# Linear attention: the inverse normaliser in three stacked bf16 parts, its spread as one bf16 product, later spread and projection steps, and the mix matrix in two banks

## The chip, the cores and the metric

The kernel runs on one core of one Trainium2 chip. The metric is the device time of one execution, in microseconds. The kernel before was run three times: 3094.87, 3097.4 and 3097.8 us, median 3097.4 us.

## What is computed

The program is a stack of eight sublayers over 2048 tokens of width 128. The change touches the first one alone, linear attention with 16 heads of 64 columns:

```python
x = x + _layernorm(_L0_attn_ref(_layernorm(x, axis=-1), ...), axis=-1)

q = split_heads(x @ Wq); k = split_heads(x @ Wk); v = split_heads(x @ Wv)
q = jax.nn.elu(q) + 1.0
k = jax.nn.elu(k) + 1.0
k_sum = k.sum(axis=2)
z = jnp.einsum('bhnd,bhd->bhn', q, k_sum)[..., None] + EPS
kv = jnp.einsum('bhnd,bhne->bhde', k, v)
out = jnp.einsum('bhnd,bhde->bhne', q, kv) / z
return out.transpose(...).reshape(...) @ Wo + bo
```

## The kernel before

Each sublayer is a phase: its own buffers and semaphores, a barrier before and behind, and between two phases a short layer norm phase. Every engine runs its instructions in the order in which they are written, and waits on semaphores. All rows of the first phase lie between 19 and 209 us of the span.

The phase (`linear_attention_phase`, from line 415) handles two batches of 1024 tokens one after the other. A batch has two stages.

**Keys and values.** For each tile of 128 tokens, TensorE multiplies by Wk (L471) and Wv (L475) into four banks `proj`, ScalarE makes exp and relu, VectorE the features, and TensorE adds key by value into `outer` (L486). GpSimd sums the keys (L650).

**Queries.** A step counter u runs over 16 units (2 halves of 512 tokens by 8 chunks of 128 feature columns, two heads in each). In the order of its step, TensorE issues up to four things, each for another unit:

- `query` (L523), u < 16: one 128x512 product into `proj` bank 0 or 1. It waits until ScalarE has read the bank two units earlier.
- `normaliser` (L535), 3 steps later: the feature sums by the key sums, which gives z for the 16 heads, in rows 32j to 32j+15 for token group j. Half 0 goes to the bank `outer`, half 1 to `small`.
- `spread` (L551), 12 steps later: z's inverse, kept in `wide`, is copied to the 64 rows of each head by a product with a 0/1 matrix `select`, into `proj` bank 2 or 3. Unit u waits until VectorE has consumed unit u-2.
- `project_out` (L566), 13 steps later: four 128x128 products of the divided features `qz` with the matrix `mix` (kv by Wo) into `yacc`.

`mixes` (L510) makes the two halves of `mix` in steps 2 and 3, both in the one bank `small`, so that the second waits for VectorE's copy (L724) of the first. In step 19 of batch 0 TensorE also makes the first keys and values of batch 1.

VectorE's steps: query features (L673), in steps 10 and 18 the inversion of a half (`invert`: add epsilon L678, reciprocal L681, four copies of 16 rows into the diagonal blocks of `wide` L685), `divide` from step 12 on (L692: `qz` = features by the spread bank), `keep_y`, and in batch 1 pieces of the layer norm of batch 0. ScalarE makes exp and relu of each query (L617, L618). GpSimd has nothing in the query stage but two roots for the layer norm.

`select` and `wide` are f32 with 128 rows. The two places that order the work:

```python
for u in range(STEPS + 13):
    ...
    if 12 <= u < STEPS + 12:
        spread(b, u - 12)
    if u >= 13:
        project_out(b, u - 13)
```

## Time and profile before

| | |
|---|---|
| three runs | 3094.87, 3097.4, 3097.8 us |
| span of the profiled execution | 3093.3 us |
| its own time | not given apart from the span; the nearest run is 1.6 us above the span, the median 4.1 us |
| TensorE busy (products) | 2694.2 us, 87% |
| VectorE busy | 2049.2 us, 66% |
| ScalarE busy | 1572.2 us, 51% |
| GpSimd busy | 1072.5 us, 35% |
| mean granted TensorE clock | 0.938 |

How to read the rows further down. A row of a timeline has its start in us from the span's start, the duration in us, engine (PE is TensorE, DVE is VectorE, ACT is ScalarE, POOL is GpSimd), line, operation, output and inputs, shapes, and the count of merged records; in brackets the idle time of the engine just before, and what ended it. An f32 product shows as two records. Recorded ends of products overlap the next start; the distance of two starts is what a product costs in a stream. A row of the stretches has start and end, length, then for PE, weight loads, DVE, ACT and POOL busy us and count, and then the granted clock as a share of full speed, the DMA share and GB/s.

### The profile page before, as it was taken

How to read it: one execution, taken by the hardware profiler on the slowest of the kernel's cores; microseconds unless marked ns; L12 is line 12 of the kernel's file. 1: busy time of each engine (PE TensorE's matmuls, PEld its weight loads, DVE VectorE, ACT ScalarE, POOL GpSimd, SP SyncE). 2: the span in 40 equal slices, each digit the busy share in tenths (PEclk: the TensorE clock that was granted, in tenths of full speed). 3: DMA queues.
4: the chain of work that ended last, by engine and by line, in shares of the span. 5: the costliest groups of instructions: out<-in, count | busy, mean ns of one | idle time of the engine just before them, and what ended most of it. 6: DMA issues, size and time to landing. Idle time of an engine off the chain costs nothing. (4 is left out here: it accounts for less than half of the span.)

```text
span 3093.3 us, 55201 instructions
## 1 busy us (share of the span) xinstructions
PE 2694.2 (87%) x21256; PEld 1684.6 (54%) x21276; DVE 2049.2 (66%) x4308; ACT 1572.2 (51%) x3080; POOL 1072.5 (35%) x784
## 2 busy tenths in 40 slices
PE   8985899999799799999998888898877899777698
PEld 4552555566676566666666566465543334335465
DVE  5668999935644665546664665566439999996554
ACT  4334788852423444434554555366456676643122
POOL 3201000001243344434443553245226777773000
PEclk9995899989899899999999899998999999998899
DMA  1000000001120200000000000000013344340000
GB/s 55 1 4 1 2 3 3 3 2 82 33 89 22 84 1 1 1 1 1 1 1 1 29 1 1 1 1 1 1 66 129 137 144 144 136 143 21 1 1 14
DMA packets 34228, 105.41 MB, mean 34 GB/s; under 512 B 3456, under 2 KB 14592, under 8 KB 33200
## 3 DMA queue, kind: packets, MB, share of 16 engines
q1 hardware_dynamic: 31952, 97.69, 9.1%
q0 software_dynamic: 2016, 4.19, 0.4%
q8 instruction: 171, 2.80, 0.4%
q14 instruction: 89, 0.73, 0.1%
HBM read 94.01 MB, written 7.86 MB: 33 GB/s over the span
## 5 line engine op out<-in xcount | busy, mean ns | idle before, releaser
L2121 POOL TENSOR_TENSOR many_probs<-many_probs,many_rinv 128x2048 f32<-128x2048 f32 (+7 forms) x128 | 269.6, 2106 | 358.8 <-DVE many_rinv L2161 358.8
L1101 DVE TENSOR_REDUCE heads_halfmax<-heads_qmajor 128x1 f32<-128x512 f32 x512 | 316.3, 681 | 32.7 <-PE heads_qmajor L962 29.4
L3509 DVE TENSOR_TENSOR_SCAN stream_state<-stream_decay,stream_state 128x512 f32<-128x512 f32 x256 | 306.3, 1233 | 0.9 <-ACT stream_decay L3341 0.5
L1066 ACT ACTIVATE weights<-heads_kmajor 128x1024 f32<-128x1024 f32 x256 | 259.2, 1026 | 71.7 <-PE heads_kmajor L974 65.7
L2090 ACT ACTIVATE many_probs<-many_score,many_negmax 128x1024 f32<-128x1024 f32 (+7 forms) x256 | 187.4, 737 | 173.1 <-DVE many_negmax L2145 173.1
L2145 DVE TENSOR_REDUCE many_negmax<-many_score 128x1 f32<-128x1024 f32 (+7 forms) x256 | 184.4, 751 | 106.0 <-PE many_score L2019 104.3
L3179 PE MATMUL stream_yacc<-stream_state,ident 128*128 128x512 f32 x512 | 249.1, 614 | 0.4 <-POOL stream_state L3471 0.4
L3341 ACT ACTIVATE stream_decay<-weights,mamba_negA 128x512 f32<-128x512 f32 x256 | 173.0, 689 | 112.5 <-DVE stream_state L3509 111.3
L3471 POOL TENSOR_TENSOR stream_state<-XN,stream_state 128x1024 f32<-128x1024 f32 x85 | 200.2, 2359 | 81.6 <-DVE stream_state L3509 81.2
L2027 PE MATMUL many_ring<-ident,many_probs 128*128 128x128 f32 x1152 | 174.6, 279 | 23.4 <-POOL many_probs L2121 6.5
L3500 DVE TENSOR_TENSOR stream_state<-stream_bspread,stream_du 128x1024 f32<-128x1024 f32 x128 | 153.2, 1197 | 46.6 <-POOL stream_du L3447 38.6
L2080 ACT ACTIVATE many_probsT<-many_ring 128x512 f32<-128x512 f32 x192 | 107.8, 561 | 137.2 <-PE many_ring L2027 137.0
L990 PE MATMUL heads_outp<-weights,heads_vaug 128*9 128x128 f32 x4096 | 161.2, 276 | 13.5 <-ACT heads_outT L1059 13.2
L2027 PEld LDWEIGHTS many_ring<-ident,many_probs 128*128 128x128 f32 x1152 | 125.1, 140 | 86.1 <-DVE many_zT L2155 32.7
L2043 PE MATMUL many_ring<-many_probsT,many_v 128*64 128x128 f32 x2304 | 153.8, 278 | 12.5 <-ACT many_probsT L2080 12.4
L2499 ACT ACTIVATE local_probs<-local_score,local_negmax,loc_norms 128x192 f32<-128x192 f32 x256 | 127.3, 507 | 68.9 <-DVE local_negmax L2514 68.8
L2015 PE MATMUL many_score<-many_kT,many_qT 64*128 64x512 f32 (+3 forms) x768 | 158.6, 517 | 1.2 <-ACT many_probs L2090 1.2
L3179 PEld LDWEIGHTS stream_yacc<-stream_state,ident 128*128 128x128 f32 x512 | 101.2, 198 | 90.0 <-issue 71.8
L3170 PE MATMUL stream_bspread<-stream_BC,stream_select 128*128 128x512 bf16 x236 | 76.2, 399 | 81.7 <-DVE stream_state L3500 74.2
L2551 POOL TENSOR_TENSOR local_probs<-local_probs,local_rowsum 128x768 f32<-128x768 f32 x64 | 93.9, 1467 | 138.4 <-DVE local_rowsum L2520 138.4
L2043 PEld LDWEIGHTS many_ring<-many_probsT,many_v 128*64 128x64 f32 x2304 | 123.2, 136 | 32.3 <-ACT many_probsT L2080 20.3
L3635 PE MATMUL grouped_gate_up<-HT,weights 128*128 128x512 f32 x272 | 130.2, 602 | 0.0
(586 smaller groups left out, 5925.5 us busy)
## 6 DMA issues: line engine op xcount, KB each, us to landing
XN<-mamba_crows SPq DMA_DIRECT2D x85, 512.0 KB, 3.6
stream_crow<-mamba_crows SPq DMA_DIRECT2D x43, 512.0 KB, 3.7
weights<-in_w_dram SPq DMA_DIRECT2D x1, 6148.0 KB, 17.3
weights<-in_w_dram SPq DMA_DIRECT2D x1, 4274.0 KB, 12.9
weights<-in_w_dram SPq DMA_DIRECT2D x1, 3296.0 KB, 10.9
swiglu_pairs<-swiglu_fetched SPq DMA_DIRECT2D x1, 2310.0 KB, 10.4
weights<-in_w_dram SPq DMA_DIRECT2D x1, 2112.0 KB, 8.2
swiglu_fetched<-swiglu_pairs SPq DMA_DIRECT2D x4, 528.0 KB, 7.3
```

What stands on the lines that cost most here:

```text
L990: last = nc.tensor.matmul(outp[32 * j:32 * j + 9, 0, c * P:(c + 1) * P], vaug[:, b * TPB + kc, 4 * c + j, :], probs_of(4 * q + j // 2 * 2 ...
L1066: nc.scalar.activation(probs_of(k).rearrange("p (a n) -> p a n", a=2), kmajor[:, at:at + 2, :], ACT.Exp, scale=SC).then_inc(exp_done, 1)
L1101: nc.vector.tensor_reduce(halfmax[:, g % 2, at, h % 2:h % 2 + 1], qmajor[:, (2 * n + j) % 3, :], AX, ALU.max).then_inc(max_done, 1)
L2027: last = nc.tensor.transpose(ring[:, k % 2, x % 4 * P:(x % 4 + 1) * P], probs[:, n % 4, x * P:(x + 1) * P], m.ident[:])
L2043: last = nc.tensor.matmul(ring[DH * h:DH * (h + 1), k % 2, 0:P], v[:, g % 2, kb, DH * h:DH * (h + 1)], probsT[:, n % 2, x * P:(x + 1) * P] ...
L2090: nc.scalar.activation(probs[:, n % 4, h * wide:(h + 1) * wide], score_of(n, h)[:, 0:wide], ACT.Exp, bias=negmax[:, n % 3, h:h + 1], accum ...
L2121: nc.gpsimd.tensor_tensor(pair, pair, rinv[:, n % 4, :].unsqueeze(2).broadcast_to([P, 2, wide]), ALU.mult).then_inc(norm_done, 1)
L2145: nc.vector.tensor_reduce(negmax[:, n % 3, h:h + 1], score_of(n, h)[:, 0:(UNITS[n][1] + 1) * P], AX, ALU.max, negate=True).then_inc(negmax ...
L3179: last = nc.tensor.matmul(yacc[:, half, :], m.ident[:], state[:, g % STATES, part(half)], start=(g % NS == 0), stop=(g % NS == NS - 1))
L3341: nc.scalar.activation(decay[:, h % DECAYS, :], delta_of(j, ch)[:, part(half)], ACT.Exp, scale=negA[:, a:a + 1]).then_inc(dec_done, 1)
L3471: nc.gpsimd.tensor_tensor(state[:, g % STATES, :], crow_of(g), state[:, g % STATES, :], ALU.mult).then_inc(hc_done, 1)
L3509: nc.vector.tensor_tensor_scan(h[:, part(half)], decay[:, (2 * g + half) % DECAYS, :], h[:, part(half)], 0.0 if half == 0 else h[:, BANK - ...
```

## The change

- `select` and `wide` become bf16 with 96 rows. VectorE splits the inverse `norm` into `high` (bf16 cast), `rest` = norm - high, `middle` (bf16 cast of rest), `low` = rest - middle. The three parts are stacked in `wide`: GpSimd copies the high part to rows 0 to 15, ScalarE `rest` (cast to bf16 in the copy) to rows 32 to 47, VectorE `low` to rows 64 to 79, four copies of 16x128 each. One bf16 product then sums the three parts as it spreads them.
- ScalarE's copies stand behind the exp and relu of query 11 for half 0, and behind query 15 for half 1. GpSimd's stand behind the key sum of the batch's last tile and, in batch 1, ahead of the last two roots.
- `spread` and `divide` run 13 steps behind the query (12 before), `project_out` 15 (13 before). `keep_y` of half 0 moves from step 21 to 24.
- The second half of `mix` goes to `proj` bank 3, and waits for the last value copy in place of the mix copy. The first spread into bank 3 waits for the second mix copy.

```diff
+    SPREAD_LAG, PROJECT_LAG = 13, 15
...
-        pick = ph.sb("pick", [P, 16])
-        select = ph.sb("select", [P, 16, DH])
+        pick = ph.sb("pick", [96, 16])
+        select = ph.sb("select", [96, 16, DH], BF16)
...
-        wide = ph.sb("wide", [P, 2, BANK])
+        wide = ph.sb("wide", [96, 2, BANK], BF16)
...
-                if 2 * b + part > 0:
-                    pe.wait_ge(mix_done, 2 * b + part)
+                    if b > 0:
+                        pe.wait_ge(mix_done, 2 * b - 1)
+                else:
+                    pe.wait_ge(val_done, 2 * TPB * (b + 1))
...
                 if c == 0:
-                    pe.wait_ge(wide_done, 4 * (2 * b + half + 1))
+                    for r in range(3):
+                        pe.wait_ge(stacked[r], 4 * (2 * b + half + 1))
...
                 elif u == 1:
-                    pe.wait_ge(val_done, 2 * TPB * (b + 1))
+                    pe.wait_ge(mix_done, 2 * b + 2)
...
+            def stack_middle(b, half):
+                act.wait_ge(split_done, 4 * (2 * b + half) + 2)
+                for j in range(4):
+                    nc.scalar.activation(wide[32:48, half, j * P:(j + 1) * P], rest[32 * j:32 * j + 16, half, :],
+                                         ACT.Copy).then_inc(stacked[1], 1)
...
                     query_parts(b, u)
+                    if u == 11:
+                        stack_middle(b, 0)
                     if b == 1 and u < 7:
                         nz.scale_tile(act, 0, u + 1)
+                stack_middle(b, 1)
...
+                if g in (TPB - 1, 2 * TPB - 1):
+                    for half in range(2):
+                        i = 2 * (g // TPB) + half
+                        pool.wait_ge(norm_done, i + 1)
+                        for j in range(4):
+                            nc.gpsimd.tensor_copy(wide[0:16, half, j * P:(j + 1) * P],
+                                                  norm[32 * j:32 * j + 16, half, :]).then_inc(stacked[0], 1)
+                            pool.wait_ge(stacked[0], 4 * i + j + 1)
...
+                nc.vector.tensor_copy(high[:, half, :], norm[:, half, :]).then_inc(split_done, 1)
+                dve.wait_ge(split_done, at + 1)
+                nc.vector.tensor_tensor(rest[:, half, :], norm[:, half, :], high[:, half, :],
+                                        ALU.subtract).then_inc(split_done, 1)
+                dve.wait_ge(split_done, at + 2)
+                nc.vector.tensor_copy(middle[:, half, :], rest[:, half, :]).then_inc(split_done, 1)
+                dve.wait_ge(split_done, at + 3)
+                nc.vector.tensor_tensor(low[:, half, :], rest[:, half, :], middle[:, half, :],
+                                        ALU.subtract).then_inc(split_done, 1)
+                dve.wait_ge(split_done, at + 4)
                 for j in range(4):
-                    rows = slice(32 * j, 32 * j + 16)
-                    nc.vector.tensor_copy(wide[rows, half, j * P:(j + 1) * P], norm[rows, half, :]).then_inc(wide_done, 1)
+                    nc.vector.tensor_copy(wide[64:80, half, j * P:(j + 1) * P],
+                                          low[32 * j:32 * j + 16, half, :]).then_inc(stacked[2], 1)
...
-                for u in range(STEPS + 12):
+                for u in range(STEPS + SPREAD_LAG):
...
-                    if u == 21:
+                    if u == 24:
                         keep_y(b, 0)
```

How the order moves. On TensorE in batch 0, from query 12 to the first projection (`lin_select` marks the spread, `lin_mix` the projection). Before:

```order
L523 MATMUL lin_proj<-HT,weights 128x512
L535 MATMUL lin_small<-lin_qry,lin_ksumcols 16x128 x4
L551 MATMUL lin_proj<-lin_wide,lin_select 128x512
L523 MATMUL lin_proj<-HT,weights 128x512
L535 MATMUL lin_small<-lin_qry,lin_ksumcols 16x128 x4
L551 MATMUL lin_proj<-lin_wide,lin_select 128x512
L566 MATMUL lin_yacc<-lin_mix,lin_qz 128x128 x4
```

With the change:

```order
L532 MATMUL lin_proj<-HT,weights 128x512
L544 MATMUL lin_small<-lin_qry,lin_ksumcols 16x128 x4
L561 MATMUL lin_proj<-lin_wide,lin_select 128x512
L532 MATMUL lin_proj<-HT,weights 128x512
L544 MATMUL lin_small<-lin_qry,lin_ksumcols 16x128 x4
L561 MATMUL lin_proj<-lin_wide,lin_select 128x512
L532 MATMUL lin_proj<-HT,weights 128x512
L544 MATMUL lin_small<-lin_qry,lin_ksumcols 16x128 x4
L561 MATMUL lin_proj<-lin_wide,lin_select 128x512
L576 MATMUL lin_yacc<-lin_mix,lin_qz 128x128 x4
```

A query and a normaliser more stand ahead of the first spread, and three spreads (two before) ahead of the first projection.

On TensorE in batch 0, steps 2 and 3, the two halves of `mix`. Before:

```order
L510 MATMUL lin_small<-weights,lin_kvT 64x128 x8
L523 MATMUL lin_proj<-HT,weights 128x512
L510 MATMUL lin_small<-weights,lin_kvT 64x128 x8
L535 MATMUL lin_outer<-lin_qry,lin_ksumcols 16x128 x4
```

With the change:

```order
L519 MATMUL lin_small<-weights,lin_kvT 64x128 x8
L532 MATMUL lin_proj<-HT,weights 128x512
L519 MATMUL lin_proj<-weights,lin_kvT 64x128 x8
L544 MATMUL lin_outer<-lin_qry,lin_ksumcols 16x128 x4
```

The second half has another bank as its output; its place is the same.

On VectorE in batch 0, the second inversion. Before:

```order
L692 TENSOR_TENSOR lin_qz<-lin_qry,lin_proj 128x512 x3
L678 TENSOR_SCALAR lin_norm<-lin_small 128x128
L681 RECIPROCAL lin_norm<-lin_norm 128x128
L685 COPY lin_wide<-lin_norm 16x128 x4
L692 TENSOR_TENSOR lin_qz<-lin_qry,lin_proj 128x512 x4
```

With the change:

```order
L730 TENSOR_TENSOR lin_qz<-lin_qry,lin_proj 128x512 x3
L705 TENSOR_SCALAR lin_norm<-lin_small 128x128
L708 RECIPROCAL lin_norm<-lin_norm 128x128
L711 CAST lin_high<-lin_norm 128x128
L713 TENSOR_TENSOR lin_rest<-lin_norm,lin_high 128x128
L716 CAST lin_middle<-lin_rest 128x128
L718 TENSOR_TENSOR lin_low<-lin_rest,lin_middle 128x128
L722 CAST lin_wide<-lin_low 16x128 x4
L730 TENSOR_TENSOR lin_qz<-lin_qry,lin_proj 128x512 x7
```

Two casts and two subtractions stand between reciprocal and copies, and three divisions of half 0 are left behind it, for two before (the merged rows also hold divisions of half 1).

## Rows read from the trace of the kernel before

**Rows 1.** Busy time by stretch; columns: busy and count per engine, granted clock.

```profile
98.00:116.00 18.00, 18.00 (x103) 12.90 (x102) 7.25 (x12) 1.08 (x2) 0.00 (x0) 1.00 0.00 1
210.00:220.00 10.00, 7.01 (x63) 6.82 (x62) 7.76 (x50) 5.95 (x15) 4.03 (x4) 1.00 0.01 2
220.00:224.00 4.00, 3.38 (x16) 3.02 (x15) 0.93 (x2) 1.28 (x4) 0.00 (x0) 0.58 0.00 0
```

**Rows 2.** Timeline of TensorE, batch 0, one step of the tail.

```profile
109.26 1.02 PE L551 MATMUL lin_proj<-lin_wide,lin_select 128*128 128x512 f32 x2
110.12 1.05 PE L566 MATMUL lin_yacc<-lin_mix,lin_qz 128*128 128x128 f32 x8
111.01 1.02 PE L551 MATMUL lin_proj<-lin_wide,lin_select 128*128 128x512 f32 x2
```

**Rows 3.** Timeline of VectorE, the same step.

```profile
110.32 0.69 DVE L692 TENSOR_TENSOR lin_qz<-lin_qry,lin_proj 128x512 f32<-128x512 f32 x1 [1.06 <-PE lin_proj L551]
```

**Rows 4.** Timeline of TensorE in the last phase: its bf16 spread.

```profile
2893.43 0.38 PE L3657 MATMUL grouped_spread<-grouped_partsT,grouped_select 96*128 96x512 bf16 x1
2893.65 1.05 PE L3669 MATMUL grouped_down<-weights,grouped_hidden 128*128 128x128 f32 x8
```

**Rows 5.** Timeline of TensorE, batch 0, up to the first spread.

```profile
77.00 0.41 PE L535 MATMUL lin_small<-lin_qry,lin_ksumcols 128*16 128x128 f32 x8
...
78.40 0.41 PE L535 MATMUL lin_small<-lin_qry,lin_ksumcols 128*16 128x128 f32 x8
79.76 1.13 PE L551 MATMUL lin_proj<-lin_wide,lin_select 128*128 128x512 f32 x2 [0.95 <-DVE lin_wide L685]
```

**Rows 6.** Timeline of VectorE, batch 0, the first inversion.

```profile
77.43 0.28 DVE L678 TENSOR_SCALAR lin_norm<-lin_outer 128x128 f32<-128x128 f32 x1
77.75 0.95 DVE L681 RECIPROCAL lin_norm<-lin_norm 128x128 f32<-128x128 f32 x1
78.74 0.97 DVE L685 COPY lin_wide<-lin_norm 16x128 f32<-16x128 f32 x4
```

**Rows 7.** Timeline of TensorE, batch 1, around the second inversion.

```profile
188.94 0.41 PE L535 MATMUL lin_small<-lin_qry,lin_ksumcols 128*16 128x128 f32 x8
...
192.47 1.16 PE L566 MATMUL lin_yacc<-lin_mix,lin_qz 128*128 128x128 f32 x8 [0.31 <-DVE lin_qz L692]
```

**Rows 8.** Timeline of VectorE, batch 1, the second inversion and what follows.

```profile
189.42 0.29 DVE L678 TENSOR_SCALAR lin_norm<-lin_small 128x128 f32<-128x128 f32 x1
...
191.73 0.69 DVE L692 TENSOR_TENSOR lin_qz<-lin_qry,lin_proj 128x512 f32<-128x512 f32 x1
```

**Rows 9.** Timeline of TensorE, the second half of the mix, batches 0 and 1.

```profile
64.79 1.09 PE L510 MATMUL lin_small<-weights,lin_kvT 64*64 64x128 f32 x16 [0.43 <-DVE lin_mix L724]
...
158.90 1.09 PE L510 MATMUL lin_small<-weights,lin_kvT 64*64 64x128 f32 x16 [0.42 <-DVE lin_mix L724]
```

**Rows 10.** Timeline of VectorE, the router: a split into bf16 parts, 128x128.

```profile
670.85 0.23 DVE L744 CAST router_parts<-router_gates 128x128 bf16<-128x128 f32 x1
671.11 0.29 DVE L745 TENSOR_TENSOR router_rest<-router_gates,router_parts 128x128 f32<-128x128 f32 x1
671.43 0.23 DVE L746 CAST router_parts<-router_rest 128x128 bf16<-128x128 f32 x1
```

**Rows 11.** Timeline of ScalarE, the next phase: six small copies.

```profile
229.88 1.30 ACT L820 ACTIVATE heads_qstack<-hprep_parts 128x128 bf16<-128x128 bf16 x6 [8.59 <-DVEq L871]
```

**Rows 12.** Timeline of GpSimd: small operations, each waiting for the one before.

```profile
309.53 0.25 POOL L1122 CAST heads_qstack<-heads_negmax 128x16 bf16<-128x16 f32 x1 [30.59 <-DVE heads_negmax L1091]
309.86 0.22 POOL L1123 TENSOR_TENSOR heads_rest<-heads_negmax,heads_qstack 128x16 f32<-128x16 f32 x1
```

**Rows 13.** One line of VectorE: copies beside GpSimd copies; ns min/median/max.

```profile
L876 DVE COPY hprep_kstack<-hprep_parts x48: 194/320/322, 229.9 to 278.7; 128x128 bf16<-128x128 bf16 x48
```

**Rows 14.** Timeline of GpSimd and VectorE, batch 1: two operations that overlap.

```profile
146.83 2.34 POOL L650 TENSOR_TENSOR lin_keytotal<-lin_keytotal,lin_key 128x1024 f32<-128x1024 f32 x1
...
148.18 1.54 DVE L668 SCALAR_TENSOR_TENSOR lin_key<-lin_featexp,lin_featrelu 128x512 f32<-128x512 f32 x1
```

More of the change, by code:

```diff
@@ L435, in linear_attention_phase @@
         norm = ph.sb("norm", [P, 2, P])
-        wide = ph.sb("wide", [P, 2, BANK])
+        high = ph.sb("high", [P, 2, P], BF16)
+        middle = ph.sb("middle", [P, 2, P], BF16)
+        rest = ph.sb("rest", [P, 2, P])
+        low = ph.sb("low", [P, 2, P])
+        wide = ph.sb("wide", [96, 2, BANK], BF16)
         qz = ph.sb("qz", [P, 3, BANK])
@@ L447, in linear_attention_phase @@
                                 "kvT_done", "total_done", "ksum_psum", "ksum_done", "mix_psum", "mix_done", "q_psum",
-                                "q_exp", "q_relu", "q_done", "z_psum", "z_kept", "norm_done", "wide_done", "spread_done",
+                                "q_exp", "q_relu", "q_done", "z_psum", "z_kept", "norm_done", "spread_done",
                                 "qz_done", "qz_used", "y_kept", "bias_psum", "bias_done", "cleared", "pick_done",
                                 "select_done"))
+        split_done = ph.sem("split_done")
+        stacked = [ph.sem(f"{x}_stacked") for x in ("high", "middle", "low")]
         nz = Normaliser(nc, m, ph, "n_", True, True, EARLY[s])
@@ L509, in mixes @@
                         rows = slice(DH * h, DH * (h + 1))
-                        last = nc.tensor.matmul(small[rows, 0, c % 4 * P:(c % 4 + 1) * P], kvT[rows, c * DH:(c + 1) * DH],
+                        last = nc.tensor.matmul((small[:, 0, :], proj[:, 3, :])[part][rows, c % 4 * P:(c % 4 + 1) * P], kvT[rows, c * DH:(c + 1) * DH],
                                                 w["Wo"][rows, c * P:(c + 1) * P], start=True, stop=True,
@@ L579, in _ @@
                         accumulate(g - 1)
-                for u in range(STEPS + 13):
+                for u in range(STEPS + PROJECT_LAG):
                     if u < STEPS:
@@ L635, in _ @@
             nc.gpsimd.memset(wide[:], 0.0).then_inc(cleared, 1)
-            for j in range(1, 4):
-                first = m.ident[:, 0:16] if j == 1 else pick[:]
-                pool.wait_ge(pick_done, j - 1)
-                nc.gpsimd.tensor_tensor(pick[:], first, m.ident[:, 32 * j:32 * j + 16], ALU.add).then_inc(pick_done, 1)
-            pool.wait_ge(pick_done, 3)
-            nc.gpsimd.tensor_copy(select[:], pick[:].unsqueeze(2).broadcast_to([P, 16, DH])).then_inc(select_done, 1)
+            for r in range(1, 3):
+                first = m.ident[0:96, 0:16] if r == 1 else pick[:]
+                pool.wait_ge(pick_done, r - 1)
+                nc.gpsimd.tensor_tensor(pick[:], first, m.ident[0:96, 32 * r:32 * r + 16], ALU.add).then_inc(pick_done, 1)
+            pool.wait_ge(pick_done, 2)
+            nc.gpsimd.tensor_copy(select[:], pick[:].unsqueeze(2).broadcast_to([96, 16, DH])).then_inc(select_done, 1)
             for g in range(BATCH * TPB):
```

17 lines of the change are left out of this document (9 added, 8 removed).

## The prediction

> **What bounds the kernel now.** The change stays inside the first phase, which ends before 209 us of 3093. Nothing outlives a phase but the weight transfers, issued at its start, so what the phase wins the whole kernel wins. So I read the phase by stretches, then the timelines of the engines at the places the change touches, then rows of other phases that show the added operations.
>
> The stretch of 18 us in the tail of batch 0, which holds nearly only spreads and projections, has TensorE busy for 18.00 us at a granted clock of 1.00, that is at 2.4 GHz, with VectorE at 7.25 [rows 1]. One step of the tail shows it: a spread starts 0.86 us before the projection, and that 0.89 us before the next spread, with no idle time on TensorE; VectorE waited 1.06 us for the spread and then divided for 0.69 [rows 2, 3]. TensorE is the bound, and in most query steps ahead of it too. It waits at three kinds of places: 0.95 us for the first spread of batch 0, whose `wide` is not ready [rows 5] (the same in batch 1), 0.31 us behind the second inversion of batch 1 [rows 7], 0.43 and 0.42 us for the second half of the mix [rows 9].
>
> **The spread.** Removed: an f32 product of 0.86 us [rows 2]. Added: a bf16 product of 96 rows by 512 columns. The last phase has that shape between the same f32 work: it starts 0.22 us before the four 128x128 products that follow [rows 4]. There are 2 batches x 16 units, so 32 x (0.86 - 0.22) = 20.5 us less on TensorE. A tail step then takes 0.22 + 0.89 = 1.11 us. Can the loop keep up? Division u waits for spread u and for projection u-3. It starts some 0.42 us after its spread and ends at 1.11, and spread u+2 and projection u need it only at 2.2: 1.1 us to spare. VectorE is busy 0.69 of 1.11. So the tail stays TensorE's, and that is why the projection was moved back.
>
> **The mix.** The second half no longer waits for the copy of the first; the value bank it takes was read long before. Its 0.43 and 0.42 us [rows 9] go. Nothing is late next: query 4 needs the relu of query 2, which is done before. Minus 0.85 us.
>
> **The inversion.** It was epsilon, reciprocal and copies: 0.32 and 0.99 from start to start, then 0.97 [rows 6]; start to the next division, 2.31 [rows 8]. Added on VectorE between reciprocal and copies: two casts at 0.26 and two subtractions at 0.32 from start to start, each waiting for the one before as here [rows 10], 1.16 us. The four copies stay four copies of 16 rows; I leave them at 0.97. Beside them:
>
> - ScalarE's four copies, by six for 1.30 [rows 11], are 0.87 us. They start once `rest` is there, 0.58 us or a little more after the reciprocal, and end before VectorE's.
> - GpSimd's four, each waiting for the one before, at 0.33 [rows 12], are 1.3 us from the reciprocal, against VectorE's 2.1.
>
> So `low` is the last part of the three, if the engines leave each other alone. They don't quite. VectorE's small copies beside GpSimd copies took 0.320 us in the median against 0.194 at the least, 0.126 more [rows 13]. GpSimd's four copies can meet up to four of VectorE's operations; I take three meetings, 0.38 us. The inversion grows by 1.16 + 0.38 = 1.54, to 3.85 us.
>
> *A rule against this.* A GpSimd addition of 2.34 us from 146.83 on overlapped a two-input VectorE operation that began at 148.18 and took 1.54 us; it ended 0.55 us after GpSimd's, so it seems to have run whole behind it [rows 14]. The Trainium skill (SBUF — State Buffer, "SBUF: two separate sides") calls the pair of ports that the two engines share "an exclusive lock, not a bandwidth split": the loser waits for the whole instruction. These rows agree with it. By that rule all four of GpSimd's copies would hold up VectorE for their whole time; it is the first rival below.
>
> **What the longer inversion costs TensorE, half 0.** VectorE begins it at 77.43 behind the features of query 10 [rows 6], as now. `wide` is complete at 77.43 + 1.31 + 1.54 + 0.97 = 81.25, the spread can go at 81.3. TensorE was free at 78.81 (79.76 less the idle 0.95 [rows 5]); the later lag puts one query and one normaliser ahead of the spread, 1.40 us by the distance of two normalisers [rows 5], so it is free at 80.21. The wait is 1.09, for 0.95: 0.14 lost per batch, 0.28 in all. ScalarE stands at its four copies until about 80.5, and with it the exp and relu of query 12; their relu ends near 81.5, query 14 follows the spread at 81.6 and needs just that. This place is tight, but covered. Without the later lag the wait would be 2.49.
>
> **Half 1.** The inversion starts 0.07 us after the last normaliser (188.94 + 0.41, against 189.42 [rows 7, 8]). Division 5 now stands behind it and ends at 0.07 + 3.85 + 0.69 = 4.61; spread 7 waits for that, so 4.65. TensorE meanwhile has spread 5 with 0.1 for the change of shape, projection 3, spread 6, projection 4: 0.32 + 0.89 + 0.22 + 0.89 = 2.32, from 0.07 before the recorded end, so 2.25. In batch 1 it waits 2.40 (0.31 now). In batch 0 the key and value products of step 19 fill 2 x 0.86 = 1.72 of it, and 0.68 is left (none now). Loss: 2.09 + 0.68 = 2.77. This is a new wait that the change makes by halving the work that had hidden the inversion. In batch 1 the two layer norm roots on GpSimd now stand behind its copies, about 1.3 us later than now; ScalarE's eight scalings then still end some 5 us before the phase.
>
> **At no cost.** The build of `select` on GpSimd lies before the first key sum. The copy of `y` at step 24 lies in VectorE's idle share of the tail; at 21 it would have waited for projection 7 with two divisions queued behind it.
>
> **The sum.** 20.5 + 0.85 - 0.28 - 2.77 = 18.3 us. The profiled span of 3093.3 becomes 3075.0. The median of the three runs stands 4.1 above that span, with its own spread of 3 us; I take the difference off the median: 3097.4 - 18.3 = **3079.1 us**.
>
> **Bounds.** Each us added to the inversion is paid at four places. Without any meeting of GpSimd and VectorE, 4 x 0.38 = 1.5 us come back: gain 19.8. Were both inversions' waits wholly hidden, 20.5 + 0.85 + 1.9 + 0.3 = 23.6. Copies from one group of rows into another have no row of this shape; below I take 0.24 each as now, above the 0.61 of a whole 512-column operation, 4 x 0.37 = 1.5 more per inversion, 5.9 in all: gain 12.4. The distance to the copies now is far the nearer one.
>
> **Rivals.**
>
> - *GpSimd and VectorE take turns for whole operations.* Four GpSimd copies at 0.25 us of work hold up VectorE 1.0 instead of 0.38: 4 x 0.62 = 2.5 us less gain, 3081.6. For it rows 14; against it rows 13, where the cost was 0.126 and not a whole copy. Chance 0.11.
> - *The stacking copies are dear*, 0.61 each: gain 12.4, 3085.0. Chance 0.05.
> - *Less waiting than I take, or a shift in the later clock.* Behind this phase the granted clock falls from 1.00 to 0.58 between two stretches near 220 us, after one with TensorE busy for only 7.01 of 10 us [rows 1]. If its falls and rises come elsewhere against the work, some us go either way; 3 us is the spread of the three runs. With full hiding 3074. Chance 0.07.
> - *The spread isn't cheaper*: bf16 between f32 products costs what f32 did. Then only the waits change: -0.85 + 0.28 + 2.77, 2.2 us slower, 3099.6. Rows 4 speak against it. Chance 0.02.
> - *Slower: the clock falls in the stage itself.* The new wait of 0.68 us in batch 0, soon after the 1.09, leaves TensorE idle more densely than before. If the granted clock fell to 1.2 GHz there, each us of its work would cost one more; it decides from 18.3 us of work on. The tail of batch 0 has 9 spreads and 11 projections left, 11.8 us; with 17 us of the key stage behind it, 28.8 - 18.3 = 10.5 us slower, 3107.9. Against it: in the present trace waits of 0.95 us left the clock at 1.00. Chance 0.02.
>
> **The numbers.** My forecast has 0.73. The range takes in the first rival, the dear copies' price and the faster rival but for its edge: 3073 to 3085.5. About 0.2% (6.2 us) is what a measurement of this kernel can tell from no change. All cases but the last two are faster by more: 0.95; within it 0.03, with the spread rival; slower 0.02.
>
> **What would show it.** In the profile after: spreads starting 0.22 us before the projection; tail steps of 1.11 us; no wait at the second mix; a first-spread wait of about 1.1 us; a wait for division 5 of about 2.4 us in batch 1 and 0.7 in batch 0; inversions of 3.85 us from epsilon to the next operation; the phase's last projection some 18 us earlier. I am wrong if the tail is paced by VectorE's divisions, if GpSimd's or ScalarE's part is the last to arrive, or if the clock leaves 1.00 before 190 us.

## The result: 22 us faster, and the profile after

| | before | changed |
|---|---|---|
| median | 3097.60 us (3094.87 to 3099.36, 4 runs) | 3075.26 us (3072.95 to 3077.75, 4 runs) |
| span of the profiled execution | 3093.3 us | 3075.7 us, its own time 3077.52 |
| TensorE busy (products) | 2694.2 us | 2672.3 us |
| VectorE busy | 2049.2 us | 2054.6 us |
| mean granted TensorE clock | 0.938 | 0.938 |

The ratio is 0.9925, with a 95% interval of 0.9913 to 0.9937. The forecast was 3079.1 in a range of 3073 to 3085.5, faster with 0.95: it holds, 3.8 us too high.

The timeline of TensorE in the changed kernel, batch 0: the two waits at the first spread, the wait for division 5, and the tail behind it, which answers to [rows 2, 5].

```profile
82.11 0.38 PE L561 MATMUL lin_proj<-lin_wide,lin_select 96*128 96x512 bf16 x1 [0.99 <-ACT lin_wide L633]
82.71 1.12 PE L532 MATMUL lin_proj<-HT,weights 128*128 128x512 f32 x2 [0.22 <-ACT lin_featrelu L628]
...
94.91 0.39 PE L561 MATMUL lin_proj<-lin_wide,lin_select 96*128 96x512 bf16 x1 [0.49 <-DVE lin_qz L730]
...
96.03 0.38 PE L561 MATMUL lin_proj<-lin_wide,lin_select 96*128 96x512 bf16 x1
96.25 1.05 PE L576 MATMUL lin_yacc<-lin_mix,lin_qz 128*128 128x128 f32 x8
97.14 0.38 PE L561 MATMUL lin_proj<-lin_wide,lin_select 96*128 96x512 bf16 x1
```

A tail step is 0.22 + 0.89 = 1.11 us, to the digit what was forecast. The second half of the mix, the same view, no longer waits [rows 9]:

```profile
64.65 1.12 PE L532 MATMUL lin_proj<-HT,weights 128*128 128x512 f32 x2
65.71 1.09 PE L519 MATMUL lin_proj<-weights,lin_kvT 64*64 64x128 f32 x16
```

VectorE's timeline of the first inversion, beside [rows 6]: 3.58 us from epsilon to the next operation at 81.93.

```profile
78.35 0.28 DVE L705 TENSOR_SCALAR lin_norm<-lin_outer 128x128 f32<-128x128 f32 x1
78.67 0.95 DVE L708 RECIPROCAL lin_norm<-lin_norm 128x128 f32<-128x128 f32 x1
79.66 0.23 DVE L711 CAST lin_high<-lin_norm 128x128 bf16<-128x128 f32 x1
79.92 0.29 DVE L713 TENSOR_TENSOR lin_rest<-lin_norm,lin_high 128x128 f32<-128x128 f32 x1
80.24 0.23 DVE L716 CAST lin_middle<-lin_rest 128x128 bf16<-128x128 f32 x1
80.50 0.36 DVE L718 TENSOR_TENSOR lin_low<-lin_rest,lin_middle 128x128 f32<-128x128 f32 x1
80.90 1.00 DVE L722 CAST lin_wide<-lin_low 16x128 bf16<-16x128 f32 x4
81.93 1.45 DVE L700 SCALAR_TENSOR_TENSOR lin_qry<-lin_featexp,lin_featrelu 128x512 f32<-128x512 f32 x2
```

The other two parts, by ScalarE's and GpSimd's timelines:

```profile
80.24 1.30 ACT L633 ACTIVATE lin_wide<-lin_rest 16x128 bf16<-16x128 f32 x4 [1.14 <-DVE lin_rest L713]
81.57 0.60 ACT L627 ACTIVATE lin_featexp<-lin_proj 128x512 f32<-128x512 f32 x1
82.06 0.59 ACT L628 ACTIVATE lin_featrelu<-lin_proj 128x512 f32<-128x512 f32 x1
...
79.69 1.38 POOL L678 CAST lin_wide<-lin_norm 16x128 bf16<-16x128 f32 x4 [19.04 <-DVE lin_norm L708]
```

GpSimd ends at 81.07, ScalarE at 81.54, VectorE at 81.90, and the spread starts at 82.11. The row of the spread names ScalarE, but ScalarE was done 0.36 us before VectorE: the name at a wait for three semaphores has to be held against the ends. Query 12's exp and relu stand behind ScalarE's copies; the relu starts at 82.06, ends at 82.65, and query 14 goes at 82.71. The batch 1 counterpart waits the same 0.99 and 0.22, and for division 5 it waits 2.11.

**How to compare two runs here.** The timed runs of one kernel lie 4 to 12 us apart, which is as much as most of the edits below are worth. Below, the *phase* runs from the start of the bias product (L571 before, L581 now) to the start of the last `Y` copy, the *part behind* from there to the end of the span. In twelve profiled executions the part behind took 2881.0 to 2890.3 us, whatever was changed ahead of it; the granted clock falls and rises in it. The two traces of the changed kernel differ by 1.6 us in the phase, all of it one fall of the clock. So the phase is the sharper measure, though each kernel but the changed one has only one trace for it. The ratios compare each run with the kernel before as timed in the same session.

| kernel | median us | ratio to before (95%) | phase us | part behind us |
|---|---|---|---|---|
| before | 3097.60 | | 189.16 | 2884.6 |
| changed | 3075.26 | 0.9925 (0.9913, 0.9937) | 171.32 | 2883.4 |
| again (the changed kernel) | 3077.82 | 0.9934 (0.9921, 0.9948) | 169.72 | 2886.8 |
| f32_late | 3094.11 | 0.9984 (0.9975, 0.9994) | 186.24 | 2881.6 |
| mix_two_banks | 3098.14 | 1.0000 (0.9991, 1.0009) | 188.18 | 2886.1 |
| bf16_early | 3091.32 | 0.9974 (0.9964, 0.9984) | 179.33 | 2881.0 |
| early_filled | 3084.35 | 0.9958 (0.9945, 0.9971) | 177.18 | 2890.3 |
| no_high_copies | 3075.85, 1 run | | 169.34 | 2884.6 |
| no_split | 3075.06, 1 run | | 168.37 | 2885.1 |
| lag_14_16 | 3080.76 | 0.9949 (0.9936, 0.9963) | 170.34 | 2886.2 |
| interleaved | 3075.70 | 0.9931 (0.9918, 0.9944) | 167.22 | 2886.6 |
| combined | 3074.36 | 0.9925 (0.9911, 0.9938) | 168.36 | 2884.8 |

Four of the phases (changed, early_filled, no_split, combined) contain one fall of the clock behind the key sums of batch 1, of 1.6 us each; it is told of at the end. Without it the phase of combined is 166.7, of no_split 166.7, of the changed kernel 169.7, the same as in `again`. So the phase gained 189.16 - 169.72 = **19.4 us**.

### The profile page after: what moved, and what is told of

Same layout as the page of the kernel before. It is cut to its first block and busy times, and to the rows that moved or that the text cites. A ratio compares the mean times of both kernels' runs of the same rounds, so it can differ in the third digit from the quotient of the medians.

```text
span 3075.7 us, 55192 instructions
## 1 busy us (share of the span) xinstructions
PE 2672.3 (87%) x21224; PEld 1677.4 (55%) x21244; DVE 2054.6 (67%) x4324; ACT 1576.8 (51%) x3096; POOL 1076.7 (35%) x799
## 3 DMA queue, kind: packets, MB, share of 16 engines
q0 software_dynamic: 2016, 4.19, 0.4%
## 5 line engine op out<-in xcount | busy, mean ns | idle before, releaser
L1028 PE MATMUL heads_outp<-weights,heads_vaug 128*9 128x128 f32 x4096 | 162.1, 277 | 13.5 <-ACT heads_outT L1097 13.2
```

The source lines that it names most:

```text
L1028: last = nc.tensor.matmul(outp[32 * j:32 * j + 9, 0, c * P:(c + 1) * P], vaug[:, b * TPB + kc, 4 * c + j, :], probs_of(4 * q + j // 2 * 2 ...
```

## The experiments

My theory: the gain is TensorE's, from the cheap spread, less waits that the longer inversion makes. Rivals: the lag alone does it, the clock punishes the waits, GpSimd's copies hold up VectorE and so set the inversion's length.

**1. The changed kernel again**, unaltered, as a scale.

> The changed kernel unaltered, timed in five rounds. The one profile of it shows the first phase 17.8 us shorter than before (from the first key product to the last copy of y), the runs' medians differ by 22.3 us. Theory one, the phase is all of it: the ratio settles at 0.9942 (17.8 of 3097) give or take 0.001, and the work behind the phase takes as long as before. Rival, some 4 us more come from behind the phase (the clock of a later stage falls at another place): the ratio stays at 0.9928 and the profile shows a later stretch some us shorter than before.

Measured: ratio 0.9934, phase 169.72, with waits of 0.99, 0.22, 0.49 and 2.12 us at the same places. What follows: the waits repeat to 0.01 us; the two medians, 2.6 us apart, do not. The interval, 0.9921 to 0.9948, holds both 0.9942 and 0.9928, so the ratio doesn't choose between the two forecasts; the part behind, 2886.8 us for 2884.6 before, is no shorter, and that speaks for the phase.

**2. The lags alone**, with the f32 spread and one mix bank.

```diff
-                for u in range(STEPS + 13):
+                for u in range(STEPS + 15):
...
-                    if 12 <= u < STEPS + 12:
-                        spread(b, u - 12)
+                    if 13 <= u < STEPS + 13:
+                        spread(b, u - 13)
...
-                    if u >= 13:
-                        project_out(b, u - 13)
+                    if u >= 15:
+                        project_out(b, u - 15)
```

> The kernel before with only the later steps: spread and division 13 behind, projection 15 behind, y kept at step 24; the spread stays f32 and the inversion as it was. Theory one, the gain is the cheaper product: only the three waits for an inversion can go, 0.95 + 0.95 + 0.31, so 2.2 us less than before, 3095 us, no wait for the first spread. Rival, the later steps are a large part of the gain: 8 us or more less.

Measured: ratio 0.9984, phase 2.9 us shorter. TensorE waits nowhere in it but at the second half of the mix. The three waits that are gone were 2.2 us; the other 0.7 us, from the new order of the products, I did not follow. Of its timeline, a spread that follows a normaliser:

```profile
85.43 1.12 PE L551 MATMUL lin_proj<-lin_wide,lin_select 128*128 128x512 f32 x2
86.39 1.05 PE L566 MATMUL lin_yacc<-lin_mix,lin_qz 128*128 128x128 f32 x8
```

What follows: the lag is worth little by itself; it takes away the old waits but for the mix, and there were few. Also, such an f32 spread takes 0.96 us from start to start, not the 0.86 of the tail [rows 2].

**3. The spread and the banks, with the old lags.**

```diff
-    SPREAD_LAG, PROJECT_LAG = 13, 15
+    SPREAD_LAG, PROJECT_LAG = 12, 13
...
-                    if u == 24:
+                    if u == 21:
```

> The changed kernel with the old steps: spread 12 behind, projection 13 behind, y kept at step 21. Theory one, the later lag hides 1.4 us of each first inversion: the first spread waits 2.4 us for its parts in each batch (0.99 now), the tail step stays 1.11 us, the whole is some 3 us slower than the changed kernel. Rival, the projection's own lag matters: the projection waits for its division in every tail step (division ends 1.1 us behind its spread), the tail step is 1.2 us or more, and the whole is 6 us or more slower than the changed kernel.

Measured: ratio 0.9974; the runs reach from 3081.86 to 3093.93 us, and the profiled one was the fastest of nine. The timeline of TensorE, its waits in both batches, and its windows (rows of stretches, as in [rows 1]) around them:

```profile
80.86 0.59 PE L561 MATMUL lin_proj<-lin_wide,lin_select 96*128 96x512 bf16 x1 [2.39 <-ACT lin_wide L633]
81.24 1.91 PE L532 MATMUL lin_proj<-HT,weights 128*128 128x512 f32 x2
...
98.39 1.16 PE L576 MATMUL lin_yacc<-lin_mix,lin_qz 128*128 128x128 f32 x8 [1.38 <-DVE lin_qz L730]
...
168.59 0.38 PE L561 MATMUL lin_proj<-lin_wide,lin_select 96*128 96x512 bf16 x1 [2.39 <-ACT lin_wide L633]
...
186.21 2.04 PE L576 MATMUL lin_yacc<-lin_mix,lin_qz 128*128 128x128 f32 x8 [3.00 <-DVE lin_qz L730]
```

```profile
79.00:85.00 6.00, 4.14 (x21) 2.14 (x22) 4.16 (x11) 3.39 (x8) 0.69 (x3) 0.72 0.00 0
170.00:174.00 4.00, 4.00 (x28) 2.36 (x27) 2.39 (x6) 1.25 (x3) 0.00 (x0) 0.67 0.00 0
186.00:190.00 4.00, 3.79 (x18) 3.63 (x19) 1.90 (x8) 0.00 (x0) 1.01 (x1) 0.57 0.01 4
```

The query behind the first wait takes 1.91 us for 1.12, the projection behind the last 2.04 for 1.16: with granted clocks of 0.57 to 0.72 in these windows, TensorE is at 1.2 GHz for much of them. Behind the wait of 1.38 us the clock stayed at 1.00. The phase is 9.6 us longer than in `again`. Its waits sum to 2.39 + 0.28 + 1.38 + 2.39 + 0.28 + 3.00 = 9.72 us, against 0.99 + 0.22 + 0.49 + 0.99 + 0.22 + 2.12 = 5.03: 4.7 us are waits. Of the other 4.9 the three falls of the clock are 4.6: from the first product behind each wait until the clock is back the products take 3.11, 4.19 and 3.74 us, where the same products take 1.73, 2.63 and 2.10 at a clock of 1.00. What follows: the waits of 2.39 us came as forecast and the tail step stayed at 1.11, but the theory's 3 us was too low. The rival's size came, 6 us or more, and not its cause; the clock is what both had left out. In this fastest trace half of the gain (9.6 of 19.4 us) is lost without the later lag, by the medians of the session 13.5 of 20.0 us (3091.32 and 3077.82, for 3097.84 before), and the lag earns about as much by keeping the clock as by hiding the wait.

**4. The mix in two banks alone.**

```diff
-                if 2 * b + part > 0:
-                    pe.wait_ge(mix_done, 2 * b + part)
+                    if b > 0:
+                        pe.wait_ge(mix_done, 2 * b - 1)
+                else:
+                    pe.wait_ge(val_done, 2 * TPB * (b + 1))
...
-                                              small[:, 0, :]).then_inc(mix_done, 1)
+                                              (small[:, 0, :], proj[:, 3, :])[u - 2]).then_inc(mix_done, 1)
```

> The kernel before with only the second half of the mix in its own bank. Theory: no wait at the second half of the mix in either batch (0.43 and 0.42 before), the first phase 0.85 us shorter, the time within the measurement's uncertainty of before. Rival: the wait only moves to the first normaliser or to query 4, and the phase is as long as before.

Measured: ratio 1.0000, phase 0.98 us shorter; both waits at the second mix are gone, the others stand at 0.95, 0.95 and 0.32. What follows: the part is worth what was forecast (0.85), and the whole time can't show it.

**5. The waits of experiment 3, filled**: two products whose result nobody reads ahead of the first spread, and one (batch 1: three) ahead of projection 6.

```diff
+            def fill(b, n):
+                pe.wait_ge(z_kept, 2 * b + 1)
+                for _ in range(n):
+                    nc.tensor.matmul(outer[:, 0, :], w["Wq"][:, 0:P], m.HT[:, 0:BANK], start=True, stop=True)
...
+                if u == 0:
+                    fill(b, 2)
...
+                if u == 6:
+                    fill(b, 3 if b else 1)
```

> The variant with the old steps (spread 12 behind, projection 13 behind), plus products that nothing reads: two 128x512 f32 products ahead of the first spread of each batch, and ahead of projection 6 one in batch 0 and three in batch 1, so that TensorE works through most of its waits of 2.39, 1.38 and 3.00 us. Theory one, the clock: those waits let the granted clock fall to half, and that, more than the waits, makes the variant 15 us slower in the median than the changed kernel. Then the clock stays at 1.00 in the query stages, the first phase takes 174 to 175 us (179.3 without the fillers, 169.7 in the changed kernel), and the median comes down from 3091 to about 3081. Rival, the waits themselves and the order cost it all: the first phase stays near 179 us, the median near 3091 or above.

Measured: ratio 0.9958 against 0.9974, median 3084.35 us for 3091.32, where 3081 was forecast. No fall of the clock at the filled places; windows of batch 0:

```profile
76.00:84.00 8.00, 7.51 (x49) 2.94 (x43) 6.37 (x16) 5.40 (x12) 1.19 (x4) 1.00 0.00 0
84.00:92.00 8.00, 7.72 (x70) 4.75 (x69) 4.16 (x7) 2.17 (x4) 0.00 (x0) 1.00 0.01 2
92.00:100.00 8.00, 7.49 (x50) 5.20 (x50) 6.04 (x14) 2.31 (x6) 1.14 (x4) 1.00 0.00 1
```

What follows: the order of the work is that of experiment 3, only the idle time is filled, and the falls are gone. So it was the idle time ahead of them that brought them, as far as one trace of each kernel can show it: three of three long waits were followed by a fall, and none of the filled ones. The phase, 177.18 with one fall of 1.6 behind the key sums, would be 175.5, forecast 174 to 175: 3.8 us shorter than in experiment 3, for 4.6 that the falls cost; the fillers themselves take a little more than the idle time that they fill (2.45 us for 2.39 ahead of the first spread).

**6. The changed kernel without GpSimd's copies.** It leaves out the high part of the inverse.

```diff
-                    for r in range(3):
+                    for r in (1, 2):
                         pe.wait_ge(stacked[r], 4 * (2 * b + half + 1))
...
                         pool.wait_ge(norm_done, i + 1)
-                        for j in range(4):
-                            nc.gpsimd.tensor_copy(wide[0:16, half, j * P:(j + 1) * P],
-                                                  norm[32 * j:32 * j + 16, half, :]).then_inc(stacked[0], 1)
-                            pool.wait_ge(stacked[0], 4 * i + j + 1)
```

> The changed kernel without GpSimd's copies of the high part (wide keeps zeros there, so the spread leaves that part of the inverse out). It measures what GpSimd costs VectorE. By the prediction's three meetings of 0.126 us the inversion falls from 3.62 to 3.24 us between its first operation and the next one; taking full turns would give 1.0 us less, 2.6; if they hardly meet, 0.2 us or less. The subtraction that took 0.36 us in all four inversions takes 0.29.

VectorE's timeline of the first inversion, to be held against that of the changed kernel above, and TensorE's two waits behind it:

```profile
79.39 0.23 DVE L712 CAST lin_middle<-lin_rest 128x128 bf16<-128x128 f32 x1
79.65 0.29 DVE L714 TENSOR_TENSOR lin_low<-lin_rest,lin_middle 128x128 f32<-128x128 f32 x1
79.98 0.97 DVE L718 CAST lin_wide<-lin_low 16x128 bf16<-16x128 f32 x4
80.98 0.69 DVE L696 SCALAR_TENSOR_TENSOR lin_qry<-lin_featexp,lin_featrelu 128x512 f32<-128x512 f32 x1
...
81.05 0.38 PE L561 MATMUL lin_proj<-lin_wide,lin_select 96*128 96x512 bf16 x1 [0.78 <-ACT lin_wide L633]
81.86 1.12 PE L532 MATMUL lin_proj<-HT,weights 128*128 128x512 f32 x2 [0.43 <-ACT lin_featrelu L628]
```

Measured: the inversion takes 3.49 us for 3.58, and the second of batch 0 3.49 for 3.72; what GpSimd's copies added is 0.07 on the second subtraction and 0.03 to 0.13 on the copies. The phase is 0.4 us shorter, and all of that comes back at division 5, whose waits are 0.26 and 1.98 for 0.49 and 2.12. At the first half nothing comes back: the spread waits 0.78 for 0.99, but query 14 waits 0.43 for 0.22, 1.21 us in sum as before. What follows: the meetings cost 0.1 to 0.2 us per inversion, not the 0.38 of the sum and far from the 1.0 of the rival. And VectorE's length alone doesn't set what the first half costs; experiments 7 and 8 show what does.

**7. The changed kernel without the split.** The casts and subtractions are left out, so that the middle and low rows hold copies of the inverse itself and not its parts.

```diff
-                act.wait_ge(split_done, 4 * (2 * b + half) + 2)
+                act.wait_ge(norm_done, 2 * b + half + 1)
...
-                nc.vector.tensor_copy(high[:, half, :], norm[:, half, :]).then_inc(split_done, 1)
...
-                nc.vector.tensor_tensor(low[:, half, :], rest[:, half, :], middle[:, half, :],
-                                        ALU.subtract).then_inc(split_done, 1)
...
-                                          low[32 * j:32 * j + 16, half, :]).then_inc(stacked[2], 1)
+                                          norm[32 * j:32 * j + 16, half, :]).then_inc(stacked[2], 1)
```

> The changed kernel without the two casts and two subtractions of each inversion: the copies to the middle and low rows read the inverse itself, so the three-part split is left out and the stacked rows aren't its parts. Theory (the remaining waits are set by the inversion's length): inversion 3.6 us becomes about 2.4, the wait for division 5 in batch 1 falls from 2.11 to about 0.9, in batch 0 from 0.49 to 0, the first spread's wait from 0.99 to about 0; the first phase is 3 to 3.5 us shorter than 169.7, about 166.4. Rival (the copies of ScalarE and GpSimd set the first spread's wait, not VectorE's chain): the first spread still waits 0.5 us or more, and less than 2.5 us comes back.

Measured: the inversion takes 2.47 to 2.52 us. The waits of TensorE that are left, in its timeline (0.61 in batch 1 too):

```profile
80.87 1.13 PE L532 MATMUL lin_proj<-HT,weights 128*128 128x512 f32 x2 [0.61 <-ACT lin_featrelu L628]
...
176.05 0.39 PE L561 MATMUL lin_proj<-lin_wide,lin_select 96*128 96x512 bf16 x1 [0.99 <-DVE lin_qz L719]
```

The waits at the first spread are gone, that for division 5 falls from 2.12 to 0.99 and in batch 0 from 0.49 to none. The phase is 168.37, or 166.7 without the fall behind the key sums, 3.0 us shorter. What follows: VectorE's chain sets the wait for division 5, one for one: the inversion is 1.12 us shorter (2.51 for 3.63) and the wait 1.13. In the first half the rival is right as to the sum. The edit also lets ScalarE's copies start one cast and one subtraction earlier, 0.58 us, and the first half's waits fall by 0.60, from 1.21 to 0.61 us at query 14. That, and not the 1.1 us by which VectorE's part is shorter, is what came back there.

**8. Lags of 14 and 16.**

```diff
-    SPREAD_LAG, PROJECT_LAG = 13, 15
+    SPREAD_LAG, PROJECT_LAG = 14, 16
```

> The changed kernel with one more step: spread 14 behind, projection 16 behind, y of half 0 kept at step 25. Theory one, a wait for an inversion costs TensorE its length less the work ahead of it: the first spread's 0.99 and query 14's 0.22 go in both batches (1.40 us more work stand ahead), the wait for division 5 goes in batch 0 (0.49) and shrinks by 0.4 in batch 1 (2.11): 3.3 us less in the first phase, 166.4 us for 169.7. Rival, the engine behind is the bound (ScalarE's copies hold query 12's relu, division 4 now also stands behind the second inversion): the waits only change place, and the first phase is within 1 us of now.

The timeline of TensorE, its waits in batch 0 (1.59 and 2.29 in batch 1):

```profile
81.45 1.12 PE L532 MATMUL lin_proj<-HT,weights 128*128 128x512 f32 x2 [1.59 <-ACT lin_featrelu L628]
...
92.79 0.39 PE L561 MATMUL lin_proj<-lin_wide,lin_select 96*128 96x512 bf16 x1 [0.49 <-DVE lin_qz L730]
```

Measured: phase 170.34, no gain, as the rival had it. The first spread no longer waits; query 14 does, for ScalarE, and division 4, now behind the second inversion, keeps spread 6 waiting. The 1.59 is the old 0.99 + 0.22 and the 0.38 that spread 0 took ahead of query 14 and now takes behind it. Query 14 starts 61.72 us behind the start of the phase in the changed kernel, in `again` and here, 61.73 in experiment 6, and 61.14 in experiment 7. What follows: the wait changed its place. What the first half costs is set by one chain, `rest`, ScalarE's four copies, exp and relu of query 12, query 14; whether VectorE's low part makes the spread wait on the way changed nothing in the sum of these runs. The next lag isn't free while ScalarE's copies stand ahead of query 12.

**9. VectorE's order around the inversions.** The first inversion starts ahead of the features of query 10, which run behind the reciprocal; division 5 runs behind the reciprocal of the second; GpSimd makes two of the four low copies. The first spread of a half waits for its parts behind its other waits (not in this cut).

```diff
                 nc.vector.reciprocal(norm[:, half, :], norm[:, half, :]).then_inc(norm_done, 1)
+                between()
...
-                for j in range(4):
+                for j in (2, 3):
...
+                    if u == 10:
+                        invert(b, 0, lambda: query_features(b, 10))
+                    if u == STEPS + 2:
+                        invert(b, 1, lambda: divide(b, u - SPREAD_LAG))
```

> The changed kernel with three edits: on VectorE the first inversion begins ahead of the features of query 10, which stand between its reciprocal and its split, and division 5 stands between reciprocal and split of the second; GpSimd makes two of the four copies of the low part; the first spread's waits for its parts come last. Theory one, the waits follow VectorE's part of the inversion: the first spread waits 0.3 to 0.5 us (0.99 now), query 14 not at all, division 5 no more, but spread 8 or projection 6 for 0.8 to 1.3 us in batch 1 (2.11 now); the first phase is 2 to 3 us shorter than 169.7. Rival: GpSimd becomes the last to deliver and the first phase is as long as now or longer.

TensorE's timeline, its waits in both batches:

```profile
80.96 0.38 PE L561 MATMUL lin_proj<-lin_wide,lin_select 96*128 96x512 bf16 x1 [0.75 <-POOL lin_wide L683]
...
162.82 0.38 PE L561 MATMUL lin_proj<-lin_wide,lin_select 96*128 96x512 bf16 x1 [0.18 <-issue]
163.61 1.12 PE L532 MATMUL lin_proj<-HT,weights 128*128 128x512 f32 x2 [0.41 <-ACT lin_featrelu L628]
...
176.41 0.39 PE L561 MATMUL lin_proj<-lin_wide,lin_select 96*128 96x512 bf16 x1 [1.70 <-DVE lin_qz L736]
```

Measured: phase 167.22, 2.5 us shorter, within the forecast; batch 0 has no wait for division 5. The places were forecast less well. In batch 0 the first spread waits 0.75 and not 0.3 to 0.5, since GpSimd's two low copies now end last, at 80.70 against 79.88 for ScalarE and 79.74 for VectorE, as the rival had it. In batch 1 it is spread 8 that waits, 1.70 us and not 0.8 to 1.3, for division 6, which stands behind the second inversion and two small operations of the layer norm. What follows: part of the loss was the order alone. GpSimd's copies meet more of VectorE's work here: in the first inversion the two casts and two subtractions take 1.45 us from start to start for 1.24, GpSimd's four copies 1.66 for 1.38.

**10. Experiments 8 and 9 together**, with ScalarE's copies behind query 12.

```diff
-    SPREAD_LAG, PROJECT_LAG = 13, 15
+    SPREAD_LAG, PROJECT_LAG = 14, 16
...
-                    if u == 11:
+                    if u == 12:
```

> The interleaved kernel with the lags 14 and 16 (25 Y blocks kept), and ScalarE's two stacked copies of the first half behind its exp and relu of query 12. Theory (the wait at the first spread comes from the copies ending late, the wait at query 14 with the longer lag comes from ScalarE's copies standing ahead of query 12, and both go when each has its place): first spread and query 14 wait at most 0.4 us each per batch instead of 0.75 and 1.59; the wait for division 5 in batch 1, 1.70 in the interleaved kernel, is shorter by the block's work that now lies ahead of it, about 1.1; first phase 165.8 us against 167.2 interleaved and 169.7 in the changed kernel; median 3 to 4 us under the changed kernel's. Rival (ScalarE's copies only move the wait on to query 15 or the first spread): phase 167 us or more, a wait of 1 us or more at a later query.

TensorE's timeline, its waits in both batches (in batch 1 the 0.18 is there too, the 0.15 not):

```profile
81.47 1.12 PE L532 MATMUL lin_proj<-HT,weights 128*128 128x512 f32 x2 [0.15 <-ACT lin_featrelu L628]
...
83.78 0.39 PE L561 MATMUL lin_proj<-lin_wide,lin_select 96*128 96x512 bf16 x1 [0.18 <-DVE lin_qz L736]
...
175.83 0.39 PE L561 MATMUL lin_proj<-lin_wide,lin_select 96*128 96x512 bf16 x1 [1.41 <-DVE lin_qz L736]
```

Measured: the big waits of the first half are gone, as the theory had it; division 5 still waits 1.41, not 1.1. Without the fall behind the key sums the phase is 166.7 us, 3.0 less than in the changed kernel, where 3.9 were forecast and the rival had 167 or more. Its waits are 1.1 us shorter than in experiment 9, the phase only 0.5; the rest I did not follow. Its ratio, 0.9925, stands beside 0.9925 and 0.9934 of the changed kernel: only the phase shows that it is the better one, the whole times don't tell them apart.

## Why the prediction was right, and where its sizes were off

- **The spread, 20.5 us.** Right in the tail: 0.22 for 0.86. Too low by about 0.9 us: the phase gained 19.4 while its waits grew from 3.06 to 5.03 us, so the products gained 21.4. I had taken the tail's price for all 32. The spreads that follow a normaliser, seven in a batch before, took 0.96 to the next start, in experiment 2 and in the trace of the kernel before (its timeline of TensorE is below), where I could have read it; at most of these places the bf16 one takes 0.22 or 0.23, so 0.74 is saved and not 0.64. Seven times 0.10 in two batches is 1.4; part of it goes again where TensorE restarts behind its new waits (the first spread takes 0.37, the query behind it 1.06 for 0.96 before).

```profile
82.02 1.13 PE L551 MATMUL lin_proj<-lin_wide,lin_select 128*128 128x512 f32 x2
82.98 1.05 PE L566 MATMUL lin_yacc<-lin_mix,lin_qz 128*128 128x128 f32 x8
```

- **The mix, 0.85.** Right: the waits went, alone worth 0.98.
- **The inversion, 3.85.** It measured 3.58 to 3.72. The split's 1.16 was right. The three meetings at 0.126 with GpSimd are the term that failed, 0.38 for 0.1 to 0.2: the meetings of [rows 13] were dearer than those here, where GpSimd copies 16 rows at a time. "Each us added to the inversion is paid at four places" holds for the two places of division 5 only; in experiment 6 the first halves got nothing back for the 0.1 us.
- **The first spread, 1.09 for 0.95.** It waits 0.99. That is 0.10 less than forecast, where the inversion is 0.27 shorter: the spread starts 0.21 us behind the last of three parts, before the change 0.05 behind its one. And ScalarE's four copies took 1.30 and not 0.87, 0.33 apiece where [rows 11] had 0.22 in rows of another shape; so query 14, "tight, but covered", was not covered and waits 0.22. By experiments 6 to 8 it is this place, and not the first spread, that sets what the first half costs. Sum per batch 1.21, a loss of 0.26 and not 0.14. "Without the later lag the wait would be 2.49": it was 2.39.
- **The second half, 0.68 and 2.40.** Measured 0.49 and 2.11, with the shorter inversion. The mechanism, a new wait because halved work no longer hides the inversion, is shown by experiment 7, and by experiment 2, where the long spreads hide the old inversion wholly.
- **The sum.** With these sizes 20.5 + 0.9 + 0.85 - 0.52 - 2.29 = 19.4 us, against 18.3 forecast; it closes because the 0.9 was taken from the phase. The profiled span was forecast as 3075.0 and is 3075.7, and that this is so close is luck: the 1.1 us that I missed in the gain, the 1.6 of a fall of the clock in that execution and the 1.2 by which its part behind was shorter, with 1.4 us later start of the phase, nearly cancel.
- **Medians.** The forecast 3079.1 stands above 3075.26 and 3077.82. A gain of 19.4 in place of 18.3 gives 3078.0 by the median that I started from; the rest, 2.7 and 0.2 us, is less than what runs of one kernel differ by, and no run tells more of it.
- **Whole-operation turns** (0.11): not so here. GpSimd's copies take 0.28 us each and fill most of the 1.38 us from 79.69 on; VectorE's first subtraction, inside that stretch, takes 0.29 us with them and without them, the second 0.36 for 0.29, and four copies cost an inversion 0.1 to 0.2 us. By the rule of the Trainium skill (SBUF — State Buffer, "SBUF: two separate sides"), a VectorE operation with two inputs in SBUF that meets a running GpSimd operation which reads SBUF is blocked until that one is done. These rows don't agree with it. Whether the lock exists and copies of 16 rows hold it only briefly, no run here tells; the long overlap of [rows 14] is there in the changed kernel too, a two-input VectorE operation of 1.56 us at 139.32 beside a GpSimd addition of 2.35.
- **The clock** (0.02): it did not fall behind the waits of the changed kernel. The windows from 82, 94 and 180 us on show 1.00, TensorE having waited 0.99 and 0.22, 0.49, and 2.11:

```profile
82.00:86.00 4.00, 3.67 (x25) 1.40 (x26) 3.48 (x6) 3.43 (x8) 0.00 (x0) 1.00 0.00 0
94.00:98.00 4.00, 3.51 (x29) 3.21 (x28) 3.14 (x6) 0.76 (x2) 0.00 (x0) 1.00 0.00 0
180.00:184.00 4.00, 3.75 (x30) 3.56 (x31) 3.33 (x12) 1.36 (x4) 1.01 (x1) 1.00 0.02 4
```

But the rival was near: waits of 2.39 and 3.00 us, in experiment 3, were followed by it. The 0.02 was fair for this kernel, and the argument for it thin, since it rested on waits of 0.95 only. One of my own signs of being wrong did come, "if the clock leaves 1.00 before 190 us": in this trace it is 0.60 from 148 to 152 us, behind the key sums, with no wait ahead of it. It cost 1.6 us there, `again` doesn't have it, and nothing in the prediction saw it.
- **Dear stacking copies** (0.05): VectorE's four took 1.00 to 1.10, little over the 0.97 that was taken. **Spread not cheaper** (0.02): refuted.

## What to carry to other kernels

When the bounding engine's work is made cheap, list what that work was hiding: here the longer inversion came out from behind the spreads with 2.6 us, and moving consumers later (the lag) was needed to keep half of the gain or more. When two engines deliver parts to a third, follow also what stands behind the delivery on each: here ScalarE's small copies held up a query, and that set the loss of the first half. Price a product next to the neighbours it will have, and copies by a row of the same shape and the same way of counting them. And where one phase is changed in a long program, measure the phase; the rest of it varied here by 9 us between traces.

## What was unexpected

- **Waits cost twice.** Waits of 2.39 and 3.00 us in experiment 3 were followed by a clock at half for some us, 4.6 us over three falls, while 1.38 in the same trace, 2.11 and 0.99 + 0.22 in the changed kernel and 2.29 in experiment 8 were not. Filling them with products that nobody reads paid 3.8 us back in the phase.
- **A fall behind the key sums, in some executions.** The eight key sums of batch 1 (16 records) are products of one column, with TensorE busy to within 0.1 us. Behind them the clock fell in four of twelve traces (changed, early_filled, no_split, combined) and not in the other eight, the same kernel once with and once without; behind the key sums of batch 0 it fell in none. One window of the changed kernel first, then of `again`:

```profile
148.00:152.00 4.00, 4.00 (x30) 2.16 (x26) 1.49 (x3) 1.81 (x5) 0.00 (x0) 0.60 0.00 0
```

```profile
148.00:152.00 4.00, 4.00 (x42) 1.83 (x44) 2.48 (x6) 2.88 (x7) 0.00 (x0) 1.00 0.01 2
```

From the first key sum to the second query behind the mix half it is 7.87 us in the one and 6.28 in the other. What decides it stays open; no run changed the key sums.
- **0.21 us from the last part to the spread**, where one semaphore had 0.05 and two (experiment 6) 0.10. That the number of waits in a row makes it is an argument, not shown.
